# A graph attention's logits: float32 tables split into three bfloat16 parts, and edge locations spread over partitions by TensorE

## The reference, cut to what matters

```python
h = (x @ W).reshape(N, HEADS, HEAD_DIM)
a_src = jnp.einsum('nhd,hd->nh', h, att_src)
a_dst = jnp.einsum('nhd,hd->nh', h, att_dst)
e = a_src[src] + a_dst[dst]
e = jax.nn.leaky_relu(e, NEG_SLOPE)
m = jax.ops.segment_max(e, dst, num_segments=N)
e = jnp.exp(e - m[dst])
denom = jax.ops.segment_sum(e, dst, num_segments=N)
alpha = e / denom[dst]
msg = alpha[:, :, None] * h[src]
out = jax.ops.segment_sum(msg, dst, num_segments=N)
```

## Time and profile before

| | |
|---|---|
| time, median of 3 runs (lowest, highest) | 6207.78 us (6199.53, 6211.03) |
| the profiled execution's own time | 6220.44 us |
| its span, first to last instruction | 6218.6 us |
| TensorE busy | 4670.9 us, 75% of the span |
| VectorE busy | 3251.7 us, 52% |
| ScalarE busy | 1580.9 us, 25% |
| GpSimd busy | 3323.7 us, 53% |
| mean granted clock of TensorE | 0.81 |

### The profile page before, as it was taken

How to read it: one execution, slowest core, us unless ns; L and a number is a source line. 1 busy time by engine, 2 the same in 40 slices (tenths; PEclk the granted TensorE clock), 3 DMA queues, 4 the chain that set the end, 5 groups by cost and what they waited for, 6 DMA issues and landing times. The chain is left out here.

```text
span 6218.6 us, 79842 instructions
## 1 busy us (share of the span) xinstructions
PE 4670.9 (75%) x20787; PEld 3717.7 (60%) x20788; DVE 3251.7 (52%) x7885; ACT 1580.9 (25%) x4023; POOL 3323.7 (53%) x3054
## 2 busy tenths in 40 slices
PE   2887487899865647699994959947546888788878
PEld 2777465677533425477773949935435666576645
DVE  5655577323344436733322147768824577577764
ACT  1000085333200007511101423337422122122221
POOL 1777686777757756500003146767144577677710
PEclk9555597999987678899995975559767899889988
DMA  3999565000169986565573648969354799699810
GB/s 94 353 353 321 166 231 160 9 1 1 26 229 338 336 266 200 170 204 187 187 247 125 212 125 267 273 225 335 107 170 131 210 259 268 198 260 265 254 46 26
DMA packets 778188, 1217.86 MB, mean 196 GB/s; under 512 B 104953, under 2 KB 551834, under 8 KB 777782
## 3 DMA queue, kind: packets, MB, share of 16 engines
q1 hardware_dynamic: 396294, 581.00, 30.4%
q0 software_dynamic: 141376, 371.74, 20.2%
q10 hardware_dynamic: 240240, 261.92, 12.0%
HBM read 845.27 MB, written 368.57 MB: 195 GB/s over the span
## 5 line engine op out<-in xcount | busy, mean ns | idle before, releaser
L2254 POOL DMA_INDIRECT max_rows<-tab,src_r x784 | 741.2, 945 | 313.7 <-issue 220.0
L385 POOL DMA_INDIRECT counts<-put_n,put_at x400 | 561.0, 1403 | 216.5 <-issue 135.1
L1884 POOL DMA_INDIRECT moe_x<-xn,slot x100 | 97.2, 972 | 816.6 <-POOLq L98 786.8
L950 POOL DMA_INDIRECT late_rows<-tab,src_a x416 | 421.8, 1014 | 173.7 <-issue 110.8
L646 POOL DMA_INDIRECT logit_rows<-tab,src_a x416 | 428.9, 1031 | 126.6 <-issue 116.9
L646 POOL DMA_INDIRECT logit_rows<-tab_kv,src_a x416 | 397.6, 956 | 177.2 <-issue 120.6
L2360 DVE TENSOR_TENSOR_SCAN run<-same,run,ps_t 128x512 f32<-128x512 bf16 x392 | 479.1, 1265 | 0.9 <-PE ps_t L2295 0.9
L765 PE MATMUL ps_a<-msg,sel 128*128 128x264 f32 (+1 forms) x1664 | 414.2, 398 | 86.1 <-DVEq L697 47.4
L927 PE MATMUL ps_b<-q,sel_t 128*128 x832 | 298.3, 524 | 238.3 <-DVE sel_t L846 238.0
L1429 PE MATMUL ps_a<-side,blocks 128*128 128x512 f32 x1950 | 460.4, 392 | 0.8 <-PE ps_a L1429 0.6
L2285 PE MATMUL ps_e<-w,att 64*128 64x256 f32 x1568 | 432.5, 421 | 22.7 <-DMA att<-in_attr_t 16.8
(11 more groups left out here) (463 smaller groups left out, 9844.0 us busy)
## 6 DMA issues: line engine op xcount, KB each, us to landing
blocks<-counts SPq DMA_DIRECT2D x390, 320.0 KB
slot_rows<-logit_rows ACTq DMA_DIRECT2D x208, 512.0 KB
edge_rows<-slot_rows SPq DMA_DIRECT2D x208, 512.0 KB
seg_rows<-back ACTq DMA_DIRECT2D x196, 512.0 KB, 5.1
slot_rows<-late_rows SPq DMA_DIRECT2D x104, 512.0 KB
sum_rows<-slot_rows SPq DMA_DIRECT2D x104, 512.0 KB, 5.7
counts<-zeros ACTq DMA_DIRECT2D x130, 320.0 KB
locs<-loc_slots SPq DMA_DIRECT2D x312, 128.0 KB, 5.4
```

Source lines behind the costliest of these rows:

```text
L385: nc.gpsimd.indirect_dma_start(out=g.counts, out_offset=bass.IndirectOffsetOnAxis(ap=g.put_at[:, j:j + 1], axis=0), in_=g.put_n[:, j:j + 1 ...
L950: self.nc.gpsimd.indirect_dma_start(out=self.rows[:, b * Q + j, :], out_offset=None, in_=self.g.tab, in_offset=bass.IndirectOffsetOnAxis(a ...
L2254: nc.gpsimd.indirect_dma_start(out=rows[:, b * Q + j, :], out_offset=None, in_=table, in_offset=bass.IndirectOffsetOnAxis(ap=g.src_r[:, n ...
```

## The change

- The table and the node columns are each split into three bfloat16 numbers that add up to the float32 one (`table`, `columns`); the one-hots are bfloat16 too. Each float32 matmul becomes three bfloat16 matmuls that add up in PSUM. Ten short VectorE instructions at the start of the phase make the parts.
- The locations are loaded once, on one partition (`rows`, 1 x 512 each, instead of 128 copies). TensorE spreads them over the partitions by a matmul with a row of ones, two for each group (`broadcast`), into PSUM (`ps_l`, `ps_s`), two groups ahead. VectorE and ScalarE make the one-hots from PSUM.
- ScalarE makes a group's `from_t` ahead of the next group's `far`.
- `LATE` goes from (66, 75) to (60, 69).

```diff
-LATE = (66, 75)
+LATE = (60, 69)
...
-        locs, slos = sb("locs", [P, Q, GP], BF16), sb("slos", [P, Q, GP], BF16)
-        sel_t, far, from_t = (sb(n, [P, 2, Q, P], F32) for n in ("sel_t", "far", "from_t"))
+        rows = sb("rows", [1, Q, 2, GP], BF16)
+        ones = sb("ones", [1, P], BF16)
+        sel_t, far, from_t = (sb(n, [P, 2, Q, P], BF16) for n in ("sel_t", "far", "from_t"))
+        table = sb("table", [P, 3, NT, H], BF16)
+        columns = sb("columns", [P, NT, 3, 2 * H], BF16)
...
                     if n >= Q:
-                        sp.wait_ge(sel_set, n - Q + 1)
-                    sp.dma_start(locs[:, b, :], g.loc_slots[n * GP:(n + 1) * GP].partition_broadcast(P)).then_inc(locs_in[b], 16)
-                    if n >= Q:
-                        sp.wait_ge(far_set, n - Q + 1)
-                    sp.dma_start(slos[:, b, :], g.slo_slots[n * GP:(n + 1) * GP].partition_broadcast(P)).then_inc(slos_in[b], 16)
+                        sp.wait_ge(spread, n - Q + 1)
+                    sp.dma_start(rows[:, b, 0, :], g.loc_slots[n * GP:(n + 1) * GP].rearrange("(a n) -> a n", a=1)).then_inc(rows_in[b], 16)
+                    sp.dma_start(rows[:, b, 1, :], g.slo_slots[n * GP:(n + 1) * GP].rearrange("(a n) -> a n", a=1)).then_inc(rows_in[b], 16)
...
                 for n in range(SG):
-                    if n + 1 < SG:
-                        measure(n + 1)
                     act.wait_ge(far_set, n + 1)
                     if n >= 2:
                         act.wait_ge(made, n - 1)
                     nc.scalar.activation(from_t[:, n % 2, :, :], far[:, n % 2, :, :], ACT.Relu, scale=-1.0, bias=1.0).then_inc(from_set, 1)
+                    if n + 1 < SG:
+                        measure(n + 1)
...
+                def broadcast(n):
+                    b = n % Q
+                    pe.wait_ge(rows_in[b], 32 * (n // Q) + 32)
+                    if n >= 2:
+                        pe.wait_ge(sel_set, n - 1)
+                        pe.wait_ge(far_set, n - 1)
+                    nc.tensor.matmul(ps_l[:, n % 2, :], ones[:], rows[:, b, 0, :], start=True, stop=True)
+                    nc.tensor.matmul(ps_s[:, n % 2, :], ones[:], rows[:, b, 1, :], start=True, stop=True).then_inc(spread, 1)
+
+                pe.wait_ge(ready, 1)
+                broadcast(0)
+                broadcast(1)
+                pe.wait_ge(thirds, 10)
...
                     for j in range(Q):
-                        nc.tensor.matmul(ps_a[:, n % 2, j * NT * H:(j + 1) * NT * H], from_t[:, n % 2, j, :], table, start=True, stop=True)
-                        ins = nc.tensor.matmul(ps_b[:, n % 2, j * P:j * P + 2 * H], sel_t[:, n % 2, j, :],
-                                               node_cols[:, ds(tiles[j], 1), :].rearrange("p a c -> p (a c)"), start=True, stop=True)
+                        for c in range(3):
+                            nc.tensor.matmul(ps_a[:, n % 2, j * NT * H:(j + 1) * NT * H], from_t[:, n % 2, j, :],
+                                             table[:, c, :, :].rearrange("p t h -> p (t h)"), start=c == 0, stop=c == 2)
+                        for c in range(3):
+                            ins = nc.tensor.matmul(ps_b[:, n % 2, j * P:j * P + 2 * H], sel_t[:, n % 2, j, :],
+                                                   columns[:, ds(tiles[j], 1), c, :].rearrange("p a c -> p (a c)"),
+                                                   start=c == 0, stop=c == 2)
                     ins.then_inc(made, 1)
+                    if n + 2 < SG:
+                        broadcast(n + 2)
...
                 def select(n):
-                    b = n % Q
-                    dve.wait_ge(locs_in[b], 16 * (n // Q) + 16)
+                    dve.wait_ge(spread, n + 1)
                     if n >= 2:
                         dve.wait_ge(made, n - 1)
-                    v.tensor_scalar(sel_t[:, n % 2, :, :].rearrange("p j e -> p (j e)"), locs[:, b, :],
+                    v.tensor_scalar(sel_t[:, n % 2, :, :].rearrange("p j e -> p (j e)"), ps_l[:, n % 2, :],
                                     g.pidx[:], None, ALU.is_equal).then_inc(sel_set, 1)
...
+                v.memset(ones[:], 1.0).then_inc(ready, 1)
...
+                v.tensor_copy(table[:, 0, :, :], a_s).then_inc(thirds, 1)
+                v.tensor_copy(columns[:, :, 0, :], node_cols[:]).then_inc(thirds, 1)
...
```

More of the change, by code:

```diff
@@ L968, in table_logits @@
         sb, ps, sem = ph.sb, ph.ps, ph.sem
-        locs, slos = sb("locs", [P, Q, GP], BF16), sb("slos", [P, Q, GP], BF16)
-        sel_t, far, from_t = (sb(n, [P, 2, Q, P], F32) for n in ("sel_t", "far", "from_t"))
+        rows = sb("rows", [1, Q, 2, GP], BF16)
[3 more added lines that the diff above has]
+        columns = sb("columns", [P, NT, 3, 2 * H], BF16)
+        left, rest = sb("left", [P, 2, NT, H], F32), sb("rest", [P, 2, NT, 2 * H], F32)
         hi_i, hi = sb("hi_i", [P, STEPS], I32), sb("hi", [P, STEPS], F32)
@@ L975, in table_logits @@
         part, total = (sb(n, [P, 2, Q, H], F32) for n in ("part", "total"))
[L976 to L980, removed]
+        ps_a, ps_b, ps_l, ps_s = (ps(n, [P, 2, 512]) for n in ("ps_a", "ps_b", "ps_l", "ps_s"))
+        rows_in = [sem(f"rows_in{b}") for b in range(Q)]
+        ready, laned, thirds, sel_set, far_set, from_set, made, chosen, parted, copied, summed, read, spread = (sem(x) for x in (
+            "ready", "laned", "thirds", "sel_set", "far_set", "from_set", "made", "chosen", "parted", "copied", "summed", "read", "spread"))
         with nc.Block() as block:
@@ L1008, in measure @@
                 def measure(n):
-                    b = n % Q
-                    act.wait_ge(slos_in[b], 16 * (n // Q) + 16)
+                    act.wait_ge(spread, n + 1)
                     if n >= 2:
                         act.wait_ge(from_set, n - 1)
-                    nc.scalar.activation(far[:, n % 2, :, :].rearrange("p j e -> p (j e)"), slos[:, b, :], ACT.Abs, bias=minus[:]
+                    nc.scalar.activation(far[:, n % 2, :, :].rearrange("p j e -> p (j e)"), ps_s[:, n % 2, :], ACT.Abs, bias=minus[:]
                                          ).then_inc(far_set, 1)
-                act.wait_ge(ready, 1)
+                act.wait_ge(ready, 2)
                 measure(0)
                 for n in range(SG):
-                    if n + 1 < SG:
-                        measure(n + 1)
                     act.wait_ge(far_set, n + 1)
@@ L1024, in _ @@
                     nc.scalar.activation(from_t[:, n % 2, :, :], far[:, n % 2, :, :], ACT.Relu, scale=-1.0, bias=1.0).then_inc(from_set, 1)
+                    if n + 1 < SG:
+                        measure(n + 1)
             @block.tensor
             def _(pe):
-                table = a_s.rearrange("p t h -> p (t h)")
+                def broadcast(n):
[10 more added lines that the diff above has]
+                pe.wait_ge(thirds, 10)
                 for n in range(SG):
@@ L1082, in leak @@
                                            ).then_inc(read, 1)
+                v.memset(ones[:], 1.0).then_inc(ready, 1)
                 v.tensor_scalar(minus[:], g.pidx[:], -1.0, None, ALU.mult).then_inc(ready, 1)
                 v.tensor_scalar(hi_i[:], g.src_a[:], 7, None, ALU.arith_shift_right).then_inc(ready, 1)
-                dve.wait_ge(ready, 2)
+                dve.wait_ge(ready, 3)
                 v.tensor_copy(hi[:], hi_i[:]).then_inc(ready, 1)
-                dve.wait_ge(ready, 3)
+                v.tensor_copy(table[:, 0, :, :], a_s).then_inc(thirds, 1)
+                v.tensor_copy(columns[:, :, 0, :], node_cols[:]).then_inc(thirds, 1)
+                dve.wait_ge(thirds, 2)
+                v.tensor_tensor(left[:, 0, :, :], a_s, table[:, 0, :, :], ALU.subtract).then_inc(thirds, 1)
+                v.tensor_tensor(rest[:, 0, :, :], node_cols[:], columns[:, :, 0, :], ALU.subtract).then_inc(thirds, 1)
+                dve.wait_ge(thirds, 4)
+                v.tensor_copy(table[:, 1, :, :], left[:, 0, :, :]).then_inc(thirds, 1)
+                v.tensor_copy(columns[:, :, 1, :], rest[:, 0, :, :]).then_inc(thirds, 1)
+                dve.wait_ge(thirds, 6)
+                v.tensor_tensor(left[:, 1, :, :], left[:, 0, :, :], table[:, 1, :, :], ALU.subtract).then_inc(thirds, 1)
+                v.tensor_tensor(rest[:, 1, :, :], rest[:, 0, :, :], columns[:, :, 1, :], ALU.subtract).then_inc(thirds, 1)
+                dve.wait_ge(thirds, 8)
+                v.tensor_copy(table[:, 2, :, :], left[:, 1, :, :]).then_inc(thirds, 1)
+                v.tensor_copy(columns[:, :, 2, :], rest[:, 1, :, :]).then_inc(thirds, 1)
+                dve.wait_ge(ready, 4)
                 dve.wait_ge(laned, 1)
```

## The result

The changed kernel takes **6152.34 us** (median of 4; 6140.39 to 6154.04), the kernel before 6208.21 us (median of 4; 6199.53 to 6211.03): a ratio of 0.9907, 95% interval 0.9895 to 0.9919. The profiled execution took 6154.04 us, with a span of 6152.2.

The account below looks back on a forecast made before the run. TensorE bounds `table_logits` before, GpSimd's gathers after: −60.7 us there and +9 us in `late_sum` give −52 us, from the median 6207.8 to 6156 us. Range 6143 to 6205 us; chance of faster 0.82.

Parts of the forecast that it names:

- TensorE bounds the stage before: In `table_logits` before the change, TensorE, busy 349 of 352 us, sets the pace at 3.41 us a group.
- TensorE's part: In `table_logits`, the new matmuls take 1.80 to 3.47 us a group, in between 2.0 to 2.5; threshold 2.92.
- rule for loads: TensorE in `table_logits`: 107 ns per 128-column weight load, so 2.57 us of loads a group, 3.0 to 3.5 with exposed spreading.
- fast path: TensorE in `table_logits`: 128 non-float32 weights load about twice as fast, giving about 2.5 us a group at the low clock.
- rivals with a full TensorE: `table_logits` stays TensorE-paced: 3.0 to 3.3 us a group (chance 0.15), or bfloat16 passes cost like float32, 3.41 to 3.47 (0.11).
- the one with dear small ones: In `table_logits`, small matmuls cost more than a pass does now: 4.05 us a group, 6284 us in all; chance 0.06.
- One sign of being wrong: In `table_logits`, the forecast is wrong if the granted clock stays at 0.50 with TensorE full.
- VectorE, 2.71 us a group: In `table_logits`, VectorE with `select` reading PSUM at 0.692 us takes 282 us for 104 groups, below GpSimd.
- GpSimd's part, the new bound: In `table_logits`, 60 groups of 4 gathers at 1.264 us take 303.4 us; the next phase's first gather comes 60.7 us earlier.
- The coupling through SyncE: In `table_logits`, stores waiting for gathers hold the loads, TensorE and VectorE to 2.92 us a group.
- ScalarE's order: In `table_logits`, `from_t` ahead of the next `far` brings no gain or loss; at most 1.2 us a group, never the bound.
- `late_sum`, +9 us: `late_sum` gathers 35 groups instead of 29, so 18 groups more run at 2.66 us instead of 2.16; bounds 0 and 20.

Follow-up runs that it names:

- doubled products: The changed kernel with every product made twice, 48 bfloat16 matmuls a group instead of 24: 6969.21 us, ratio 1.0082, when the kernel before took 6907.42 us.
- LATE (66, 75): The changed kernel with the old shares of gathers, 66 groups in `table_logits` and 9 in `segment_max`: 6179.99 us, ratio 0.9944.
- (58, 67): The changed kernel with 58 groups of gathers in `table_logits` instead of 60, 9 in `segment_max`: 6162.88 us, ratio 0.9908.
- slow group of runs: The last four follow-up kernels, variants of the changed kernel, run when the kernel before took 6907.42 us: 6868.28 to 6969.21 us.

## Why the prediction was right

6156 us was predicted and 6152 measured; 52 us of gain from the sum, 56 from the medians. That the two times lie within 4 us is in part luck: in a later group of runs the medians were 6162 and 6220, and two terms of the sum were off in opposite ways. The gain is steadier, 56 and 58 us. By its steps:

- **TensorE bounds the stage before.** Shown: six groups fewer to gather left T at 365.77 (−1.6 us), with TensorE busy 330 of 330.
- **TensorE's part, 1.80 to 3.47 us a group, 2.0 to 2.5 taken.** Measured about 2.5, at the clock 0.50. The weights' 128 columns don't show any longer: a step's six matmuls take 0.38 to 0.40 us, where six of the former passes would take 0.64. By the rule for loads that the prediction set against the change ("TensorE: Matmul & The Clock Gate", section "LDWEIGHTS (loading the stationary operand)", of the Trainium skill) six loads alone take 0.64 us. The traces contradict that rule for bfloat16 weights and agree with the fast path of the same page's "Weight-path perf modes". The 2.5 us, with TensorE waiting for VectorE, rule out the rivals with a full TensorE, and the 0.38 us for six matmuls the one with dear small ones; doubled products (0.055 us a matmul) agree. One sign of being wrong that the prediction named did nearly appear: the clock stayed at 0.50 with TensorE busy 19.32 of 20 us near the start. It was a poor sign, since the pace there was VectorE's, busy 20.00 of 20. The spreading was put at 0.9 us and costs 1.0 where nothing hides it.
- **VectorE, 2.71 us a group.** Measured 2.68. `select` takes 0.746 us, not 0.692, and the rest is a little shorter.
- **GpSimd's part, the new bound: 303.4 us.** Shown by LATE (66, 75) and (58, 67). It was mis-sized by 3.4 us: 240 gathers took 300.0 (3698.99 to 3999.03), 1.25 each and not 1.264, as a gather's mean is 0.947 us instead of 0.964. The barrier behind it took 1.3 us more (4.65 against 3.3), which hides part of that: −60.7 was predicted for the stage, −62.7 measured.
- **The coupling through SyncE, 2.92 us a group.** This step failed as worded, without harm to the sum. SyncE did wait for gathers (131.3 us in 43 places), but VectorE ran at 2.68 us for 200 us before any of it showed (20.00 of 20 busy at 3900) and lost 6% of its time near the end (18.75 of 20). The lead of six groups in the stores' condition and the ring of four are eaten up only slowly, by 2.89 − 2.68 = 0.21 us a group (300.0/104 = 2.89). TensorE's waits for `rows` are 15.7 us in 7 places, 7.8 of it at the stage's start, and not a pace. Three kernels agree on this. The lead lasted about 73 groups here, to 3899.95, which used up some 15 us. With 66 groups to gather (330.0/104 = 3.17, so 0.49 a group) TensorE first waits again at 3804.49, about 37 groups in, or 18 us of lead. With 58 (290.5/104 = 2.79, 0.11 a group, 12 us in the whole stage) it waits for `rows` only at the start, and T is still 10.0 us shorter. So the coupling is real but comes late, and gathers would have ended the stage without it.
- **ScalarE's order: "no gain, no loss; were the cover gone, it is 1.2 us a group at most and never the bound".** Wrong, and unseen in the total because the change makes it right. The old order takes 4.14 us a group against 2.68, 1.46 more, and turns the gain into a loss of 1.1%. The step counted ScalarE's own time (1.2 us) as if it lay beside TensorE's. With spread locations it stands in one ring with the products and the spreading, and the ring's sum counts: 4.14 us.
- **`late_sum`, +9 us.** Measured +9.6, but one profiled execution says less than that: with the same shares of gathers and the same `late_sum`, L is 285.5 to 295.1 in the six traces outside the slow group of runs, against 279.4 and 280.4 with the old shares, so +5 to +16. The last gather starts 255.6 us after the stage's first (4328.55 − 4072.99), before the change 207.8 us after (4352.77 − 4144.94). So 47.8 us more run at the slower pace, of which 1 − 2.16/2.66 is lost: 9.0 us. The pace itself in the changed kernel, by windows of TensorE's L1231 with and without gathers:

```profile
core 0: us, PE busy (x) PEld busy (x), PEclk, DMA share, GB/s
4170.00:4330.00 160.00, 120.55 (x467) 87.88 (x468) 0.97 0.92 325
...
4330.00:4360.00 30.00, 25.75 (x106) 18.70 (x106) 1.00 0.68 235
```

467/8 = 58.4 groups in 160 us are 2.74 us a group, and 106/8 = 13.3 in 30 us are 2.26. That the transfers of the gathers cause the slower pace is argued from the DMA share, 0.92 against 0.68; no run took them away from that stage, and the granted clock differs a little too (0.97 against 1.00).

The gain, split: the parts make the stage GpSimd's, and are worth nearly all of it together with LATE. The spreading adds at most some 5 us that these runs can't tell from none, and makes ScalarE's order a condition. Open are the cause of the slower condition, and what the old order costs with copied locations in an undisturbed run, which wasn't tried.

## What to carry to other kernels

When an engine that is full is made faster, price the next one by its own list, instructions times pitch: here 240 gathers at 1.25 us gave the new end to within 1%. Then move work off that new bound in the same step (LATE). Here the faster logits alone gained 0.56%, the move alone lost 0.14%, and both together gained 0.93%: the move pays only once GpSimd is the bound. An operand that an engine now makes instead of a transfer ties its consumer into a ring; walk once around it in issue order and add all the durations before calling any of them hidden.

## What the runs showed of the hardware

- Small bfloat16 matmuls with 128-column weights, half of them with 100 columns and half with 8: six take 0.38 to 0.40 us and twelve 0.66 at the clock 0.50, 0.055 to 0.067 each on average; a float32 one took 3.41/8 = 0.427 in the same place.
- The granted clock stayed at 0.50 with TensorE busy 390 of 390 us (float32 with spreading) and 330 of 330 (before with LATE (60, 69)), while `late_sum` has 0.97 to 1.00 at 75% to 86% busy. In the changed kernel's `table_logits`, with TensorE busy 251 of 280 us, it was 0.50 as well.
- The kernel before took 6208, 6215 and 6220 us in three groups of runs and 6907 in a fourth, on a chip with the same number as the group of 6215. The cause isn't known.
